# Routing and scattering of a mixture of experts, tile by tile inside attention instead of in a stage of its own

## The reference

```python
h = patches @ W.T + b
h = h + diff_attention(layernorm(h))      # 16 heads, two softmaxes each, causal, head norm, projection
x = layernorm(h)
gates = softmax(x @ Wg.T); scores, inds = top_k(gates, 2); scores /= sum(scores)
y = sum over the 2 chosen experts of scores * down_e(silu(gate_e(x)) * up_e(x))   # 16 experts, hidden 128
shared = down(silu(x @ Ws_gate.T) * (x @ Ws_up.T))                                # hidden 512
h = h + y + sigmoid(x @ Wsg.T) * shared
```

## Time and profile before

| | us |
|---|---|
| median of 3 runs (419.13, 424.42, 424.20) | 424.2 |
| the profiled execution: its own time | 418.47 |
| its span, first to last instruction | 416.5 |
| PE busy / DVE / POOL / ACT | 350.7 / 272.6 / 253.7 / 217.3 |
| mean granted TensorE clock | 0.944 |

### The profile page before, as it was taken

The page is one execution under the profiler, slowest core; times in us unless marked ns, Lnnn a source line. Parts: engine busy times, 40 slices in busy tenths (PEclk is TensorE's granted clock), DMA queues, the critical chain, the costliest instruction groups (busy, mean ns, idle before and its releaser), DMA issues.

```text
span 416.5 us, 10603 instructions
## 1 busy us (share of the span) xinstructions
PE 350.7 (84%) x3418; PEld 317.5 (76%) x3419; DVE 272.6 (65%) x666; ACT 217.3 (52%) x554; POOL 253.7 (61%) x432
## 2 busy tenths in 40 slices
PE   3969998999999999999989877869996988899200
PEld 3869997888888888888878777869985987789100
DVE  4588446466766667678788747966762666676275
ACT  4424435567677777777677735224431554454040
POOL 5666745046566665676567871677772466777462
PEclk9989999899999999999999999969998899999755
DMA  7622664566364545664400000983125344541194
GB/s 253 192 57 82 139 134 103 66 116 108 78 98 116 108 97 64 120 111 133 140 2 2 2 1 2 354 303 102 52 78 153 98 135 128 153 130 54 40 302 122
DMA packets 33345, 47.18 MB, mean 113 GB/s; under 512 B 4538, under 2 KB 26750, under 8 KB 32528
## 3 DMA queue, kind: packets, MB, share of 16 engines
q1 hardware_dynamic: 24670, 29.12, 29.9%
q0 software_dynamic: 4864, 11.71, 8.6%
q10 hardware_dynamic: 3762, 5.72, 4.7%
HBM read 23.59 MB, written 15.34 MB: 93 GB/s over the span
## 4 chain that ended last, share of the span: by engine, by line
POOL 35%; issue 23%; PE 21%; DVE 11%; DMA 6%; ACT 2%; SPq 1%; POOLq 0%; DVEq 0%
PE bank L1162 9%; POOL slots_x L620 8%; POOL on L525 4%; PE bank L1393 3%; POOL att L533 3%; DMA xr<-xt 3%; POOL x_l L494 2%; PE bank L1357 2%; POOL rs L502 2%; POOL wsh_l L596 2%; POOL ao L556 2%; PE pair L1256 2%; POOL parts L507 2%; POOL picked L640 2%; DMA yt<-picked 1%
## 5 line engine op out<-in xcount | busy, mean ns | idle before, releaser
L1256 PE MATMUL pair<-vx,PT 113*113 113x128 f32 x512 | 68.2, 276 | 1.5 <-ACT raw L764 1.5
L1256 PEld LDWEIGHTS pair<-vx,PT 113*113 113x113 f32 x512 | 60.4, 177 | 2.7 <-issue 2.0
L969 DVE TENSOR_REDUCE smax<-bank 128x8 f32<-128x392 f32 x64 | 36.0, 563 | 38.1 <-PE bank L1235 38.0
L525 POOL TENSOR_TENSOR on<-raw,rz 128x256 f32<-128x256 f32 x32 | 19.9, 621 | 60.1 <-DVE rz L1027 60.1
L640 POOL DMA_INDIRECT picked<-by,bid x40 | 39.4, 984 | 24.3 <-DVE by L1140 14.6
L1245 PE MATMUL bank<-cs,Sm 114*113 114x114 f32 x256 | 41.6, 285 | 4.9 <-DVE Sm L977 4.8
L771 ACT ACTIVATE PT<-bank 113x456 f32<-113x456 f32 x64 | 35.2, 550 | 14.3 <-PE bank L1245 13.1
L620 POOL DMA_INDIRECT slots_x<-hn2x,slot_u x32 | 33.6, 1050 | 11.9 <-issue 9.1
L1245 PEld LDWEIGHTS bank<-cs,Sm 114*113 114x113 f32 x256 | 30.2, 177 | 8.2 <-DVE Sm L977 6.3
L977 DVE TENSOR_TENSOR Sm<-bank,smax 128x392 f32<-128x392 f32 x64 | 35.8, 559 | 0.5
L1174 PE MATMUL bank<-wt_h,x_h 128*98 128x256 f32 x96 | 29.0, 302 | 7.2 <-DVE wt_l L888 6.5
(11 more groups left out here) (188 smaller groups left out, 1111.6 us busy)
## 6 DMA issues: line engine op xcount, KB each, us to landing
slots_x<-pad POOLq DMA_DIRECT2D x8, 642.5 KB, 7.5
bx<-slots_x SPq DMA_DIRECT2D x40, 128.5 KB, 2.1
Qs<-parts SPq DMA_DIRECT2D x48, 98.0 KB
Ks<-parts SPq DMA_DIRECT2D x48, 98.0 KB
we_raw<-we SPq DMA_DIRECT2D x4, 1024.0 KB, 7.9
xr<-xt ACTq DMA_DIRECT2D x13, 294.0 KB, 3.2
we_d<-we SPq DMA_DIRECT2D x1, 2048.0 KB, 8.9
yt<-picked SPq DMA_DIRECT2D x10, 196.0 KB
```

Source lines behind the costliest of these rows:

```text
L525: G.tensor_tensor(on[:].rearrange("p b m d -> p (b m) d"), raw[b][:].rearrange("p b m n -> p (b m) n")[:, :, 0:16], bc(rz[b][:].rearrange( ...
L969: V.tensor_reduce(smax[u % 2][:], score_of(u), AX.X, ALU.max).then_inc(maxed, 1)
L1256: last = T.matmul(bank[4 + b][0:JT, m * 2 * VN:(m + 1) * 2 * VN].rearrange("p (j n) -> p j n", j=2), PT[b][:, m, 0:JT], vx[i % NVX][:, :, ...
```

## The change

- `slots_x` becomes one region of REG = 1568 + 128 rows per expert. A token's row then needs only the count of its expert over earlier tiles, `run`, which DVE carries along (it starts at expert number times REG).
- So each tile is routed alone: top-2 moves to lag 22; `one_hot` (23, DVE, 3 instructions), two small count matmuls (23, PE), `ahead` (24, ACT copies them from PSUM), `places` (25, DVE, 2) and `slot_rows` (26, DVE, 3).
- POOL issues tile t's two scatters in the slots `FIRST_AT` and two slots later `SECOND_AT`; the second waits for the first to land and rewrites the id column of that tile. By the formula tiles 0 to 6 fall in slots 27 to 53 and tiles 7 to 15 in slots 65 to 89: 65, 67, 69, 71, 73, 75, 79, 83, 87 for the first. The powers move into slots 82 (`ez`) and 86 (`ed`) of POOL.
- LAST grows by 6. Shared products 5, 6 and 7 and shared downs 0, 1, 2 move into slots 80 to 88; in slot 86 DVE waits for `ez` and makes sig. The loop then runs v = 8 to 15, with downs 3 to 10 and a split from v = 9 on (the eighth split behind the loop).
- Downs 11 to 15 (BESIDE = 11) follow behind the blocks; yt moves to where the expert weights lie.
- The pads written early go away. When all counts are known, SP writes one pad block behind each expert's last row (16 DMAs at rows from registers, and one spare block). SP loads each block at a row from a register.
- DVE's routing behind the slots shrinks to counts of 16 numbers and the blocks' rows and experts (`rows`, `woff`).

```diff
-        slots_x = nc.dram_tensor("slots_x", (NBLK * BLK, ROW), F32, kind="Internal").ap()
+        slots_x = nc.dram_tensor("slots_x", (SPARE + BLK, ROW), F32, kind="Internal").ap()
...
-        DRAINED = 5
-        FIRST_SPLIT = 7
+        DRAINED = 8
+        FIRST_SPLIT = 9
+        BESIDE = 11
-        LAST = 4 * (NT - 1) + 24
+        LAST = 4 * (NT - 1) + 30
+        def first_at(t):
+            return 4 * t + 27 if t < 7 else max(4 * t + 27, 51 + 2 * t)
+        FIRST_AT = {first_at(t): t for t in range(NT)}
+        SECOND_AT = {first_at(t) + 2: t for t in range(NT)}
+        DOWN_AT = {86: 0, 87: 1, 88: 2}
... (SP)
-            sp.wait_ge(padded, 16 * NT // 2)
+            sp.wait_ge(prow_known, 1)
+            for e in range(E):
+                if e % BX == 0:
+                    rows_of(prow, e, 0, SPARE - BLK)
+                sp.dma_start(slots_x[bass.ds(at[e % BX], BLK), :], pad[:]).then_inc(padded, 16)
... (load_block)
-                sp.dma_start(bx[b % BX][:], slots_x[b * BLK:(b + 1) * BLK, :]).then_inc(bx_in[b % BX], 16)
+                sp.dma_start(bx[b % BX][:], slots_x[bass.ds(at[b % BX], BLK), :]).then_inc(bx_in[b % BX], 16)
... (POOL, end of each slot)
+            def scatter(k, t):
+                pool.wait_ge(slot_known, t + 1)
+                pool.wait_ge(hn2_done, t + 1)
+                pool.wait_ge(ids_made, 2)
+                if k == 1:
+                    pool.wait_ge(scattered[0], 16 * (t + 1))
+                    G.tensor_copy(hn2x[:].bitcast(U32)[:, t:t + 1, D], ids[:, 1, t:t + 1]).then_inc(ids_moved, 1)
+                    pool.wait_ge(ids_moved, t + 1)
+                G.indirect_dma_start(out=slots_x, out_offset=bass.IndirectOffsetOnAxis(ap=slot_u[:, k, t:t + 1], axis=0),
+                                     in_=hn2x[:, t, :], in_offset=None).then_inc(scattered[k], 16)
-                if u % 6 == 5 and u // 6 < NT // 2:
-                    pad_rows(u // 6)
+                if u in SECOND_AT:
+                    scatter(1, SECOND_AT[u])
+                if u in FIRST_AT:
+                    scatter(0, FIRST_AT[u])
+                if u == 82:
+                    pool.wait_ge(logit_done, NT)
+                    G.tensor_tensor(ez[:], inverse_euler[:], logits[:, :, E], ALU.pow).then_inc(e_exp, 1)
+                if u == 86:
+                    pool.wait_ge(gate_diff, 1)
+                    G.tensor_tensor(ed[:], euler[:], dl[:], ALU.pow).then_inc(e_exp, 1)
... (DVE: one_hot at the start of a slot, places and slot_rows at its end)
+            def one_hot(t):
+                dve.wait_ge(topped, 2 * t + 2)
+                V.tensor_copy(ixf[:], ix8[:, t, 0:TOPK]).then_inc(place_step, 1)
+                dve.wait_ge(place_step, 5 * t + 1)
+                V.tensor_tensor(oh[:], ..., ALU.is_equal).then_inc(place_step, 1)
+                dve.wait_ge(place_step, 5 * t + 2)
+                V.tensor_tensor(both[:], oh[:, 0], oh[:, 1], ALU.add).then_inc(both_done, 1)
+            def places(t):
+                dve.wait_ge(counts_kept, t + 1)
+                V.tensor_tensor(place[:], ahead[:, 0], run[:], ALU.add).then_inc(place_step, 1)
+                V.tensor_tensor(chosen_at[:], oh[:], ..., ALU.mult).then_inc(place_step, 1)
+            def slot_rows(t):
+                V.tensor_tensor(run[:], ahead[:, 1], run[:], ALU.add).then_inc(run_done, 1)
+                V.tensor_reduce(slotr[:], chosen_at[:], AX.X, ALU.add).then_inc(place_step, 1)
+                V.tensor_copy(slot_u[:, :, t], slotr[:]).then_inc(slot_known, 1)
... (DVE, slot 86 and on)
+                if u == 86:
+                    dve.wait_ge(e_exp, 1)
+                    V.tensor_scalar(ez1[:], ez[:], 1.0, None, ALU.add).then_inc(routing, 1)
+                    V.reciprocal(sig[:], ez1[:]).then_inc(weights_known, 1)
+                if u - 1 in DOWN_AT:
+                    shared_down(DOWN_AT[u - 1])
... (DVE, the loop behind the routing chain)
-            for v in range(DRAINED, NU + DOWN_LAG):
-                if DRAINED + 2 <= v < NU:
-                    shared_hidden(v)
-                    shared_low(v)
-                if 0 <= v - FIRST_SPLIT < NG:
+            for v in range(DRAINED, NU):
+                shared_hidden(v)
+                shared_low(v)
+                if 0 <= v - FIRST_SPLIT:
                     split_expert(v - FIRST_SPLIT)
                 shared_down(v - DOWN_LAG)
+            split_expert(NG - 1)
... (PE)
+                if (t := tile_at(u, 23)) is not None:
+                    pe.wait_ge(both_done, t + 1)
+                    T.matmul(bank[7][0:TT, E + 1:2 * E + 1], up_bf[0:TT, 0:TT], both[:], start=True, stop=True)
+                    T.matmul(bank[7][0:TT, 2 * E + 1:3 * E + 1], one_bf[0:TT, 0:TT], both[:], start=True, stop=True).then_inc(counted, 1)
... (PE, behind the blocks)
+            pe.wait_ge(b_hT, NBLK)
+            for t in range(BESIDE, NT):
+                shared_down(t)
```

More of the change, by code:

```diff
@@ L141, in build @@
         woff = keep("woff", [1, NBLK // BX + 1, 2 * BX], I32)
+        pad = keep("pad", [128, ROW])
+        ixf = keep("ixf", [TT, TOPK])
+        oh = keep("oh", [TT, TOPK, E], BF16)
+        both = keep("both", [TT, E], BF16)
+        ahead = keep("ahead", [TT, 2, E])
+        place = keep("place", [TT, E])
+        chosen_at = keep("chosen_at", [TT, TOPK, E])
+        slotr = keep("slotr", [TT, TOPK])
+        run = keep("run", [TT, E])
+        prow = keep("prow", [1, E], I32)
+        rows = keep("rows", [1, NBLK], I32)
         one_bf = keep("one_bf", [128, 128], BF16)
@@ L234, in build @@
         hs_l = [la(f"hs_l{n}", [128, SB, SH], F32R) for n in range(2)]
+        ya = Zone(late.at, ceiling).take
         we_h = la("we_h", [128, EGU], F32R)
@@ L445, in _, with rows_of @@
                 sp.dma_start(we_raw[:, cols], we[:, cols]).then_inc(we_in[n], 16)
+            regs = [SP.alloc_register(f"row{n}") for n in range(BX)]
+            at = [None] * BX
+            def rows_of(table, n0, low, high):
+                SP.load(regs, table[0:1, n0:n0 + BX])
+                for n in range(BX):
+                    at[n] = SP.snap(regs[n], min_val=low, max_val=high)
             def load_block(b):
+                if b % BX == 0:
+                    rows_of(rows, b, 0, SPARE)
                 if b >= BX:
@@ L1033, in slot @@
                     V.tensor_scalar(ms2[:], ms[:], 1.0 / 16.0, EPS, ALU.mult, ALU.add).then_inc(ms2_done, 1)
+                if (t := tile_at(u, 22)) is not None:
+                    top2(t)
+                if (t := tile_at(u, 25)) is not None:
+                    places(t)
+                if (t := tile_at(u, 26)) is not None:
+                    slot_rows(t)
                 if u in LOW_AT:
@@ L1047, in _ @@
                 slot(u)
-            dve.wait_ge(topped, 2 * NT)
-            done = [0]
+            done = [1]
             def link(ins):
@@ L1081, in _ @@
[L1081 to L1086 removed]
+            link(V.tensor_tensor_scan(cumb[:], cs[0:1, C_ONE:C_ONE + E], nblk[:], 0.0, ALU.mult, ALU.add))
+            numbers = cs[0:1, C_BLK:C_BLK + NBLK]
@@ L1098, in _ @@
             V.tensor_tensor(w2[:], w1[:], ed[:], ALU.mult).then_inc(weights_known, 1)
-            link(V.tensor_scalar(ez1[:], ez[:], 1.0, None, ALU.add))
-            V.reciprocal(sig[:], ez1[:]).then_inc(weights_known, 1)
-            shared_hidden(DRAINED + 1)
-            shared_low(DRAINED + 1)
             def split_expert(n):
@@ L1336, in shared_down @@
                                                      for b in range(SB)]).then_inc(sh_y, 1)
-            for v in range(DRAINED, NU + DOWN_LAG):
-                if v < NU:
-                    shared_product(v, 0)
-                    shared_product(v, 1)
+            for i in range(NT + 1):
+                step(i)
+            slot(0)
+            for i in range(NT + 1, NT + 4):
+                step(i)
+            for u in range(1, LAST):
+                slot(u)
+            for v in range(DRAINED, NU):
+                shared_product(v, 0)
+                shared_product(v, 1)
                 shared_down(v - DOWN_LAG)
```

220 lines of the change are left out of this document (99 added, 121 removed).

## The result

The changed kernel takes 445.5 us (median of four runs, 444.3 to 452.3) against 421.7 for the one before (four runs beside it): a ratio of 1.0575 with a 95% interval of 1.047 to 1.068. I had forecast 423 and a range of 411 to 433.

The account below looks back on a forecast made before the run. The first block waits for DVE's eighth expert-weight split, delayed through `ez` by POOL's drain: 315.4 plus 2.5 for attention gives 317.9 against 318.84, -0.9. That makes 417.6 us profiled, 423 on the median; range 411 to 433.

Parts of the forecast that it names:

- The bound behind `ez`: After POOL's power `ez`: the first block waits for DVE's last expert-weight split, not for scatters; eighth piece at 315.4.
- The loop of 3.64: Shared-product rounds v = 8 to 15: each takes 3.64 us, set by DVE's ring with ACT, not by PE.
- 29.1 to the eighth piece: From `shared_hidden(8)` to the eighth expert-weight piece: eight rounds, one split coming back behind round 15, 29.1 us.
- the chain of 6.2: DVE's routing operations behind the slots, ahead of `shared_hidden(8)`: four large and some fourteen small operations, 6.2 us.
- the pads behind SP's other work: 17 pad issues on SP, 12 us, ended by 298, ahead of block loads near 306: hidden by 8 us.
- The five downs behind the blocks: Downs 11 to 15: 7.1 us on PE, hidden in DVE's idle time; cost 0, up to 6 at half clock.
- the term for attention: Routing and scatters within attention: about 0.25 us a tile over 11 tiles, taken as 2.5 us, bounds 0 and 6.6.
- My upper bound: Attention: 6.6 us, 0.6 a tile, if PE's count matmuls waiting for the one-hot add as much again.
- In the drain the chain: Last tiles: POOL's scatters, roots and landing waits in order delay `ez` to 276.7, and DVE waits for it.
- The faster one: Rival: POOL's backlog in the drain holds nobody up, `ez` is done in time; 413 to 415 us, chance 0.20.
- The slower one: Rival: scatters run 1.0 us longer each, delaying `ez` and attention; 443 us, 433 if half are slow; chance 0.15.
- The Trainium skill's rule that I weighed: Advises against hiding GpSimd-issued DMA under VectorE work; by its figures the 14 scatters ahead of `ez` give an estimated 30 us.

Follow-up runs that it names:

- both costs away: Changed kernel with PE summing the one-hot rows instead of DVE's addition, and second scatters four slots behind their firsts, not two: 417.8 us.
- the kernels with the seconds later: Changed kernel with second scatters four slots behind their firsts, not two: 434.4 us; the same with DVE's one-hot addition also moved to PE: 417.8 us.
- the experiment on one operand: Changed kernel with DVE's addition of the two one-hot rows written as a maximum reduction over one operand: 436.4 us.
- with the counts later: Changed kernel with PE's count products one slot later, behind `weigh`, in bank 4; attention values not the reference's: 442.4 us.

## Why the prediction was wrong

**The bound behind `ez` was right, the last stretch in part by luck.** In the changed kernel the last scatter went out at 328.4, and the first block waited until 354.4 for the last split and not for scatters. The loop of 3.64, 29.1 to the eighth piece (28.7), the chain of 6.2 (6.1, from 319.50 to 325.63), PE idle ahead of its first block, and the pads behind SP's other work (the last 16 issued by 330.9, block loads from 347.3) all came as argued. That the whole stretch agrees to half a microsecond is partly chance: from the end of `ez` to `shared_hidden(8)` it took 11.0 us where I had 9.6, since PE's last down there took 2.86 and not 1.41, at the lower clock level behind a wait of 3.08, and from the eighth piece to the end 96.1 where I had 97.7. The five downs behind the blocks hid in the wait for the last rows, as forecast: DVE's sums for them end at 431.4, the first final sum could start at 433.0. With both costs away `shared_hidden(8)` came at 294.5 and the eighth piece was done at 323.2, where my sum with attention's term has 288.8 and 317.9.

**The step that failed is the term for attention, 2.5 us with bounds of 0 and 6.6.** It measured 28.9. I counted eight small operations at their length in the earlier trace rows, which was taken where POOL does little, and laid them into the idle times of the earlier trace rows. Their count was right: without the other costs routing takes 1.2 us over tiles 4 to 12, 0.15 a tile where I had 0.25. Their length was not: the addition took 1.05 beside POOL's work in place of 0.17, and other instructions of the same kind are held too (`run`, 0.50 in place of 0.16 at most tiles). With PE's waits behind it and its slower clock that makes 14.7 us of tiles 4 to 12 (96.2 less 81.5), of which the eight additions themselves are 9.9 (11.2 us in place of 1.3), and some 3 of tiles 0 to 4 (46.6 less 43.6). My upper bound held PE's wait for the one-hot, but priced it as another 0.35 a tile. The second part is POOL's wait for firsts that land behind the stacks, which I didn't count in attention at all: 7.8 us where the addition is away (89.3 less 81.5), 4 beside it. The third is PE's stall: 5.8 us with the low clock behind it (49.4 less 43.6), 2.3 where the clock stayed at 1.00 (46.1 less 43.8). Nothing in the trace of before announced it.

**In the drain the chain was right, its waits were too short and too few.** Ahead of `ez` I had POOL wait 1.5 us each for the firsts of tiles 12 and 13 to land; there were five waits of 9.6 us together, the longest 5.54. Those 6.6 us more are the 6.5 by which `ez` came late: 45.2 us after tile 12, not 38.7. Without its two waits my sum gives 35.7, and the kernels with the seconds later took 34.9 and 34.2. Two more waits, 5.5 us together, stand behind `ez`.

**The rivals.** The faster one, that POOL's backlog holds nobody up, is refuted: relieving it gave 11.1 us. The slower one had the size nearly right, 433 to 443, and the mechanism wrong: scatters at their slow length didn't come (median 1.008 us, longest 1.41). Here it was GpSimd's ordinary arithmetic that held VectorE's, and no rival had that direction. The Trainium skill's rule that I weighed ("SBUF — State Buffer", "Summary: rules for kernel authors") speaks of VectorE holding up what GpSimd issues; these spans don't show it. The 620 and 3100 ns of that page of the Trainium skill are the times of a whole DMA, which I took for those of its issue. The section of the Trainium skill quoted with the experiment on one operand speaks of both directions, and I had not applied it to 16 columns.

## What to carry to other kernels

Price a small VectorE operation by where it will stand: with two operands in SBUF beside a busy GpSimd it cost what GpSimd's next one to three instructions took (1.08 to 2.28 us here for 0.17), and a wait behind it in another engine's order multiplies that by the tiles. Write it as a reduction over one operand, or let TensorE's accumulation do the sum; a copy or a scaling with one operand is no such cure by these traces. Read the longest of a group as well as its mean: hn2x had its 1.96 beside 0.75 in the trace of before. Put a step that waits for a DMA far enough behind the issue that the wait is met. Compare stretches between marks of one trace and not only ends: here three separate costs of 2 to 15 us lay in one stretch, and the input stage alone moved by 9 us between the kernels' profiles.

## What the hardware showed that I had not expected

- A held VectorE instruction can lose more than one turn: the addition of 192.66 waited through the root and the squares; one of 1.77 us (237.98) through the root and a split of a shared weight, one of 2.28 (263.71) through root, split and squares.
- A conversion with one operand was held too: `slot_u`, two columns, took 0.40 us in attention and 0.17 in the drain; with the counts later it took 0.17 everywhere. Why is not tested.
- Padding PE's stream with 128 waits took a stall of 1.6 to 3.0 us away in all three kernels; one of them was faster by more than the spread (418.0 to 411.2 us), most of that in its input stage.
- TensorE's granted clock fell behind four of PE's waits in tiles 4 to 12 of the changed kernel (3.75, 1.60, 1.62 and 1.58 us): 13.7 us of that stretch ran at the lower level, nothing of it in the kernel before and in that with neither cost.
- The time to the first hn2x, on code that the edits leave alone but for the shift and a semaphore, was 109.5 to 118.6 us; in the longest, PE waited 3.1 us for a stack of keys (until 77.0 us) and had a granted clock of 0.89 from 75 to 119 us.
